# Fused convolution-attention, attention and expert layers: first two weight splits in place, norms and routing later, residual rows and last scatter reordered

## What is computed

```python
# 1: group norm, 1x1 attention over the 1024 points, residual
xn = group_norm(x, 32 groups) * gn_weight + gn_bias
q, k, v = split(qkv_w @ xn + qkv_b)
x = out_w @ (softmax(q.T @ k / 16) @ v.T).T + out_b + xn
# 2: tokens (4, 1024, 256); attention behind residual MLPs
t = tokens(x); n = layernorm(t)
q, k, v = [(n + silu(n @ W1) @ W2) @ aW for each of q, k, v]
t = t + softmax(q @ k.T, over the queries) @ v @ Wout
# 3: mixture of 8 experts, the two likeliest of each token
n = layernorm(t); m = layernorm(n) * ln_g + ln_b
p = softmax(m @ gate_w); c = p where in the top two, else 0
t = t + n + sum_e c[:, e] * (gelu(m @ w1[e] + b1[e]) @ w2[e] + b2[e])
```

## Time and profile before

| what | value |
|---|---|
| median of 3 runs (lowest to highest) | 1194.27 us (1192.0 to 1194.72) |
| profiled execution, its own time | 1192.62 us |
| its span, granted TensorE clock | 1190.9 us, 0.991 |
| PE, DVE, ACT, POOL busy | 95%, 65%, 47%, 21% |
| live expert steps start at, last product ends at | 708.2 us, 1166.2 us |
| HBM traffic over the span | 71 GB/s |

### The profile page before, as it was taken

How to read it: one execution, slowest core, us unless ns; L and a number is a source line. 1 busy time by engine, 2 the same in 40 slices (tenths; PEclk the granted TensorE clock), 3 DMA queues, 4 the chain that set the end, 5 groups by cost and what they waited for, 6 DMA issues and landing times. The chain is left out here.

```text
span 1190.9 us, 24660 instructions
## 1 busy us (share of the span) xinstructions
PE 1137.0 (95%) x8066; PEld 1057.9 (89%) x8067; DVE 777.2 (65%) x1876; ACT 554.1 (47%) x1002; POOL 254.9 (21%) x311
## 2 busy tenths in 40 slices
PE   6999999999999999999999988999899999999995
PEld 5898898888997988998988887998899999999894
DVE  5676376785475676476764679577877667766662
ACT  3533354533343532345433457677666345554442
POOL 3010000100140100231000413236433332323331
PEclk9999999999999999999999999999999999999998
DMA  5001000110010110010000361348675254345338
GB/s 173 1 1 36 1 1 1 37 36 1 15 63 2 36 36 1 33 44 19 18 1 1 108 218 24 58 117 232 198 202 130 48 129 120 61 117 124 56 59 287
DMA packets 70631, 84.65 MB, mean 71 GB/s; under 512 B 11664, under 2 KB 62096, under 8 KB 70544
## 3 DMA queue, kind: packets, MB, share of 16 engines
q1 hardware_dynamic: 57104, 66.22, 17.7%
q0 software_dynamic: 13440, 17.32, 8.1%
HBM read 55.31 MB, written 29.25 MB: 71 GB/s over the span
## 5 line engine op out<-in xcount | busy, mean ns | idle before, releaser
L1719 PE MATMUL ps<-w2s,hs 128*128 128x256 f32 x1728 | 251.1, 280 | 19.2 <-DVE hs L1685 16.2
L1719 PE MATMUL ps<-xt,w1s 128*128 128x256 f32 x1746 | 256.1, 282 | 1.2 <-issue 1.1
L1719 PEld LDWEIGHTS ps<-w2s,hs 128*128 128x128 f32 x1728 | 221.8, 188 | 25.0 <-DVE hs L1685 14.6
L1719 PEld LDWEIGHTS ps<-xt,w1s 128*128 128x128 f32 x1746 | 224.9, 188 | 1.9 <-issue 1.8
L1037 ACT ACTIVATE h<-ps,b1t 128x256 f32<-128x256 f32 x288 | 137.2, 478 | 127.2 <-PE ps L1719 86.2
L771 POOL DMA_INDIRECT acc_rows<-y_w,now_s x72 | 119.0, 1652 | 167.4 <-ACT y_w L1055 112.0
L1683 DVE CAST hs<-h 128x256 fp32r<-128x256 f32 x288 | 87.8, 305 | 95.1 <-ACT h L1037 53.9
L1685 DVE TENSOR_TENSOR hs<-h,hs 128x256 fp32r<-128x256 f32 x288 | 123.6, 429 | 9.9
L1719 PE MATMUL ps<-xs,wh 128*128 128x512 f32 x384 | 121.4, 397 | 1.8 <-issue 1.7
L1719 PEld LDWEIGHTS ps<-vk,pr 128*128 128x128 f32 x768 | 96.2, 190 | 4.7 <-DVE pr L1539 2.5
L1719 PE MATMUL ps<-vk,pr 128*128 128x256 f32 x768 | 97.4, 282 | 1.8 <-DVE pr L1539 1.8
(11 more groups left out here) (248 smaller groups left out, 1725.3 us busy)
## 6 DMA issues: line engine op xcount, KB each, us to landing
w1r<-in_w SPq DMA_DIRECT2D x13, 1024.0 KB
w2r<-in_w SPq DMA_DIRECT2D x13, 1024.0 KB
xg<-sorted_rows SPq DMA_DIRECT2D x38, 272.0 KB
b2t<-in_b SPq DMA_DIRECT2D x37, 128.0 KB
xn<-in_x SPq DMA_DIRECT2D x4, 1024.0 KB, 4.9
acc_rows<-r_out SPq DMA_DIRECT2D x4, 1024.0 KB, 5.1
rows<-acc_rows SPq DMA_DIRECT2D x8, 512.0 KB, 5.6
out_tokens<-cols_out SPq DMA_DIRECT2D x8, 512.0 KB
```

Source lines behind the costliest of these rows:

```text
L1719: ins = t.matmul(out, left[l], right[r], start=first and n == 0, stop=last and n == 2, **more)
```

## The change

1. `w1s`, `w2s` of both sets now lie first in memory; `in_lo` are fp32 names for the places of the four `lo` halves. `whole_weights` loads the weights of steps 0 and 1 straight into them, `in_place` copies `hi` and subtracts in place. `EARLY` splits all 16 pieces in the last image, at chunks 1 to 7; on DVE they stand before `max2(i + 2)` instead of behind it. Step 0 splits nothing (`chunks(i, n, False)`). SP waits for the last scores before it loads into `w1r`, `w2r`, which now lie over `xs`, `qs` and `ks`.
2. `table_a1` and `table_a2` move from chunks 0 and 1 of the last second attention to the projections, between `slots` and `weigh`.
3. The tail's tables in the expert steps move later: statistics from step 0 to 0 and 1, affines from 1 to 1 and 2, the rest by about one step; the sends of sorted rows and six of nine pads too.
4. `stream` of images 0 to 2 moves from before `hi1(0)` and chunk 1 to chunks 1, 2, 5, 6; `tail_stats(b - 1, 1)` from chunk 0 to 1.
5. ACT tests `fresh` in the unrolled steps too.
6. POOL's `scatter(s)` and `note_step(s + 2)` stand at the end of step `s`; before, `scatter(s - 1)` and `note_step(s + 1)` stood there, and the last scatter behind the loop.

```diff
--- before.py
+++ after.py
@@ -246,11 +246,18 @@
-        w1s, w2s = [halves("w1s0", [P, KC, FF])], [halves("w2s0", [P, FC, C])]
+        here = ExitStack()
+        in_lo = []
+        for n in range(4):
+            sb(f"past_hi{n}", [P, KC * FF], F32, here)
+            in_lo.append(sb(f"in_lo{n}", [P, KC * FF], F32, here))
+        here.close()
+        w1s, w2s = [], []
+        for n in range(2):
+            w1s.append(halves(f"w1s{n}", [P, KC, FF]))
+            w2s.append(halves(f"w2s{n}", [P, FC, C]))
         w1r = es("w1r", [P, 2, KC * FF])
         w2r = es("w2r", [P, 2, FC * C])
-        w1s.append(halves("w1s1", [P, KC, FF]))
-        w2s.append(halves("w2s1", [P, FC, C]))
         y_w = es("y_w", [P, 2, SUB, C])
@@ -410,31 +417,33 @@
         CNT = NT * E
-        EARLY = {4: (0, 1), 5: (2, 3), 6: (4, 5), 7: (6, 7)}
+        EARLY = {1: (0, 1), 2: (2, 3), 3: (4, 5, 6), 4: (7, 8), 5: (9, 10), 6: (11, 12, 13), 7: (14, 15)}
...
-        STATS_AT = {(0, 1): 0, (0, 3): 1}
-        NORMAL_AT = {(0, 6): 0, (1, 1): 1}
-        AFFINE_AT = {(1, 1): (0, 0), (1, 2): (0, 1), (1, 5): (1, 0), (1, 6): (1, 1)}
-        TURN_AT = {(1, 5): 0, (2, 0): 1, (2, 3): 2, (2, 6): 3}
-        COLUMNS_AT = {(2, 0): 0, (2, 3): 1, (2, 6): 2, (3, 1): 3}
-        GATE_TILES_AT = {(3, 2): (0, 1), (3, 3): (2, 3), (3, 4): (4, 5), (3, 5): (6, 7)}
-        READ_AT = (3, 7)
-        TOPS_AT = {(4, 0): (0, 1, 2), (4, 1): (3, 4, 5), (4, 2): (6, 7)}
-        CHOOSE_AT = (4, 3)
-        RANKS_AT = (4, 5)
-        EXP_AT = (4, 7)
-        SLOTS_AT = (5, 0)
-        WEIGH_AT = (5, 1)
-        TABLE_AT = {(5, 2): 0, (5, 4): 1, (5, 6): 2, (9, 2): 3}
-        ROWS_AT = {5: (0,), 6: (1, 2, 3), 7: (4, 5), 8: (6, 7)}
+        RESIDUAL_AT = {1: (0, 1), 2: (2, 3), 5: (4, 5), 6: (6, 7)}
+        STATS_AT = {(0, 5): 0, (1, 3): 1}
+        NORMAL_AT = {(1, 2): 0, (1, 7): 1}
+        AFFINE_AT = {(1, 6): (0, 0), (2, 0): (0, 1), (2, 3): (1, 0), (2, 6): (1, 1)}
+        TURN_AT = {(2, 4): 0, (2, 7): 1, (3, 2): 2, (3, 5): 3}
+        COLUMNS_AT = {(2, 7): 0, (3, 2): 1, (3, 5): 2, (4, 0): 3}
+        GATE_TILES_AT = {(4, 1): (0, 1), (4, 2): (2, 3), (4, 3): (4, 5), (4, 4): (6, 7)}
+        READ_AT = (4, 6)
+        TOPS_AT = {(4, 7): (0, 1, 2), (5, 0): (3, 4, 5), (5, 1): (6, 7)}
+        CHOOSE_AT = (5, 2)
+        RANKS_AT = (5, 4)
+        EXP_AT = (5, 6)
+        SLOTS_AT = (5, 7)
+        WEIGH_AT = (6, 0)
+        TABLE_AT = {(6, 1): 0, (6, 3): 1, (6, 5): 2, (9, 2): 3}
+        ROWS_AT = {6: (0,), 7: (1, 2, 3), 8: (4, 5), 9: (6, 7)}
         STREAM_AT = {(4, 0): 0, (4, 2): 1, (5, 1): 2, (5, 5): 3, (6, 1): 4, (6, 5): 5, (7, 1): 6, (7, 5): 7}
-        PADS_AT = {6: (0, 1), 7: (2, 3, 4), 9: (5, 6, 7, 8)}
+        PADS_AT = {7: (0, 1, 2), 8: (3, 4, 5), 9: (6, 7, 8)}
         ROWS_OUT_AT = 8
@@ -518,6 +527,13 @@
+            def whole_weights(n, e):
+                sp.dma_start(in_lo[2 * n][:, :].rearrange("p (k f) -> p k f", k=KC),
+                             w1_d[bass.ds(e, 1)].rearrange("e p k f -> (e p) k f")).then_inc(w1_in[n], 16)
+                sp.dma_start(in_lo[2 * n + 1][:, :].rearrange("p (f c) -> p f c", f=FC),
+                             w2_d[bass.ds(e, 1)].rearrange("e p f c -> (e p) f c")).then_inc(w2_in[n], 16)
@@ -560,13 +576,14 @@
-            weights(0, expert(0))
-            biases(0, expert(0))
+            for n in range(2):
+                whole_weights(n, expert(n))
+            for n in range(2):
+                biases(n, expert(n))
             sp.wait_ge(rows_free, B)
...
             gather(1, 1, True)
-            weights(1, expert(1))
-            biases(1, expert(1))
+            sp.wait_ge(s2_mm, B * NT)
@@ -762,7 +779,7 @@
-            def scatter(s, n, first):
+            def scatter(s, n):
@@ -775,13 +792,11 @@
                     s = i * 2 + n
-                    if not (isinstance(i, int) and s == 0):
-                        scatter(s - 1, 1 - n, isinstance(i, int) and s == 1)
-                    if not (isinstance(i, int) and s == 0):
-                        note_step(s + 1, 1 - n, (i if n == 0 else i + 1))
+                    scatter(s, n)
+                    note_step(s + 2, n, i + 1)
                     if isinstance(i, int):
-                        if s in ROWS_AT:
-                            send_rows(B - 1, ROWS_AT[s])
+                        if s + 1 in ROWS_AT:
+                            send_rows(B - 1, ROWS_AT[s + 1])
@@ -800,7 +815,6 @@
                     steps(i)
-            scatter(final_step(pool), 1, False)
@@ -896,8 +910,6 @@
                 else:
-                    for j in range(4):
-                        stream(b - 1, j)
                     hi1(0)
@@ -906,8 +918,8 @@
                         hi1(i)
-                    if not first and i == 1:
-                        for j in range(4, NT):
+                    if not first:
+                        for j in RESIDUAL_AT.get(i, ()):
                             stream(b - 1, j)
@@ -962,15 +974,21 @@
                         for piece in EARLY.get(i, ()):
-                            w_piece(0, 0, 0, piece)
+                            in_place(piece // 8, piece % 8)
+            def in_place(n, f):
+                if f % 4 == 0:
+                    act.wait_ge((w1_in, w2_in)[f // 4][n], 16)
+                c = slice(f % 4 * 512, (f % 4 + 1) * 512)
+                hi = (w1s, w2s)[f // 4][n][0][:, :, :].rearrange("p a b -> p (a b)")
+                a.copy(hi[:, c], in_lo[2 * n + f // 4][:, c]).then_inc(ws_act, 1)
...
-                first = isinstance(s, int) and s < 2
                 if f % 4 == 0:
                     act.wait_ge((w1_in, w2_in)[f // 4][n], at(u, 16, 16))
-                    if not first:
-                        act.wait_ge((h_mm, y_mm)[f // 4], at(s, FC, -FC))
+                    act.wait_ge((h_mm, y_mm)[f // 4], at(s, FC, -FC))
                 c = slice(f % 4 * 512, (f % 4 + 1) * 512)
@@ -1015,8 +1033,8 @@
                     act.wait_ge(b_in[n], at(i, 32, 32))
-                    if isinstance(i, int):
-                        chunks(i, n, True)
+                    if isinstance(i, int) and s == 0:
+                        chunks(i, n, False)
                     else:
@@ -1056,9 +1074,11 @@
+            act.wait_ge(tab_a, 1)
             for i in range(LOOP_AT):
+                if i == LOOP_AT - 1:
+                    act.wait_ge(tab_b, 1)
                 steps(i)
-            act.wait_ge(tab_b, 1)
             with act.Fori(LOOP_AT, PAIRS) as i:
@@ -1476,7 +1496,7 @@
                         max1(i + 2)
-                    if not first and i == 0:
+                    if not first and i == 1:
                         tail_stats(b - 1, 1)
@@ -1524,6 +1544,9 @@
                             slots(b - 1, RANK_BANK, 0)
+                            if last:
+                                table_a1()
+                                table_a2()
                         if gi == RANK_AT + 2:
@@ -1562,20 +1585,24 @@
                         lo2(i)
+                    if last:
+                        for piece in EARLY.get(i, ()):
+                            in_place(piece // 8, piece % 8)
                     if i + 2 < NT:
                         max2(i + 2)
-                    if last:
-                        if i == 0:
-                            table_a1()
-                        if i == 1:
-                            table_a2()
-                        for piece in EARLY.get(i, ()):
-                            w_piece(0, 0, 0, piece)
                     if not last:
...
+            def in_place(n, f):
+                dve.wait_ge(ws_act, 8 * n + f + 1)
+                c = slice(f % 4 * 512, (f % 4 + 1) * 512)
+                hi, lo = [a[:, :, :].rearrange("p a b -> p (a b)") for a in (w1s, w2s)[f // 4][n]]
+                v.tensor_tensor(lo[:, c], in_lo[2 * n + f // 4][:, c], hi[:, c].bitcast(F32),
+                                ALU.subtract).then_inc(ws_dve, 1)
```

## The result

The changed kernel takes 1195.56 us (median of 19 runs, 1193.21 to 1197.78), the kernel before 1192.00 beside it (19 runs); the measured ratio is 1.0039, interval 1.0029 to 1.0049. (All ratios here are the measured ones with their intervals; the quotient of two medians can differ from them by 0.001, here it is 1.0030.) I had forecast 1187.0 and faster with a chance of 0.83: it is slower than before, and 8.6 us above the forecast. The profiled execution took 1197.78 us, its span 1196.1 against 1190.9 before. It is the slowest of the 19, 2.2 us above the median, so the 5.2 us between the two spans overstate the difference somewhat.

A forecast was written before the change was run, and what follows sets the result against it. PE, busy 95% of the span, was taken as the bound, so only its waits count. The terms summed to -6.2 us, 1192.6 to 1186.4; half a microsecond added gave 1187.0, range 1184.5 to 1191.5 (chance 0.66).

The forecast's parts named there:

- Residual rows: First attention, images 1 to 3: moving the streams removes three PE waits for `lo1`, -2.7 us (0 to -2.7).
- The step table: First scores of the second attention: PE waits +3.0 us for the `u_read` memset, and a lower clock adds +1.6.
- End of the last image: Early splitting of both first weights shortens PE's wait there and keeps the clock up: -2.0 us (+1 to -3.4).
- Steps 0 to 2: First expert steps: less DVE splitting and statistics work cuts PE's loss from 8.7 to about 3, -5.0 us (-2.5 to -7.2).
- Later steps: Routing runs one step later and `table_b` fills step 6, leaving DVE no slack step behind it: +0.5 us (0 to +2).
- sends and pads: Sorted rows and pads move towards step 12, which reads them; the read comes 4.6 us later: +1.0 us (0 to +4).
- rival 3: Step 12's rows a full step late: PE waits 8.0 us and the clock falls, 1195.6 us, slower; chance 0.06.
- The loop: ACT's branch on `fresh` and its dropped copies: both set at 0, bounds -1 and +2.8 us.
- Last scatter: End of kernel: POOL's last scatter issues 0.85 us after the last `y_w` ends, -2.6 us (-2.0 to -2.7).

The follow-up runs named there:

- e4: The kernel before with only POOL's scatter and note moved as in the change; ratio 1.0008 to the kernel before.
- e10: The kernel before with only ACT's branch on `fresh` in unrolled steps 1 to 11; ratio 0.9998 to the kernel before.
- e11: e9 with the nine pads in two groups, five at key 7 and four at key 9; ratio 0.9953 to the kernel before.
- e1: The changed kernel with SP loading step 11's biases ahead of its wait for sorted rows and pads; 0.9994 to the kernel before, 1191.47 us.
- e20: The changed kernel with SP loading biases of step s+1 ahead of rows of step s+2 in every step; ratio 0.9942 to the kernel before.
- e18: e9 with norms, routing, row sends and pads at their old steps, and biases ahead of rows in every step; 0.9903 to the kernel before.
- e15: e9 with biases of step s+1 loaded ahead of rows of step s+2 in every step; ratio 0.9912 to the kernel before.
- e19: e18 with POOL's rotated order of scatter and note; ratio 0.9888 to the kernel before, 1179.89 us.
- e12: e9 with 16 unused register loads on POOL ahead of the loop; ratio 1.0014 to the kernel before.
- e16: e15 with 16 unused register loads on POOL ahead of the loop; ratio 0.9928 to the kernel before.
- e9: The changed kernel with step 11's biases first, the table's first parts behind the memset and POOL's old order; 0.9945 to the kernel before.
- e2: The changed kernel with POOL's sends of sorted rows done by one step earlier; ratio 1.0010 to the kernel before.

## Why the prediction was wrong, by its steps

- **Residual rows, -2.7**: right; alone 3.0 us. The waits for `pr` of the first attention are gone.
- **The step table, +3.0 and +1.6**: right. The rows, as the earlier trace rows, with a window of the products behind the wait:

```profile
651.13 0.06 DVE L1553 MEMSET spare<- 128x1 f32 x1
...
651.35 4.58 PE L1746 MATMUL ps<-qs,ks 128*128 128x512 f32 x12 [2.81 <-DVE spare L1553]
...
652.00:656.00 4.00, 4.00 (x13) 3.13 (x12) 0.03 (x1) 0.00 (x0) 0.00 (x0) 0.57 0.00 0
...
698.36 3.00 PE L1746 MATMUL ps<-vk,pr 128*128 128x256 f32 x24 [0.62 <-DVE pr L1562]
```

PE waits 2.81 (forecast 3.0), and the clock falls to a mean of 0.57 in the window behind: the twelve products take 4.58 us where they took 2.91, 1.7 more (forecast 1.6). Moved behind the memset it gives back 3.6 to 4.3 us of the 4.6 that I had counted.
- **End of the last image, -2.0**: right, rather more. PE's last two waits are 0.62 and 0.49 us where the one of 1.81 stood, and the first group of 24 products behind them took 3.00 us, against 4.60: this is the 2.99 of the full level that I had estimated. The stretch to turn 0 gained 3.7 where -0.1 was forecast; of this up to 2 us is the scatter of the stretch itself: e4 and e10, which change nothing ahead of turn 0, had it at 702.7 and 703.5, before at 704.9.
- **Steps 0 to 2, -5.0 (-2.5 to -7.2)**: -3.6, within the bounds. The early split carries it (2.6), the spreading adds 1.0, less than I gave to the norms. The turns are 10.3, 10.5 and 15.7 us apart, where I had 10.5, 13 and 13: step 1 gives back all, step 2 almost nothing.
- **Later steps, +0.5**: +1.2 up to turn 11. In step 9 it is more (17.4 against 14.5), which I did not work out; e11 points to the full DMA engines. The neighbours give most of it back.
- **The step that failed: sends and pads, +1.0 (0 to +4), with rival 3.** This term looked at the rows alone. I checked when PE turns them, found 3.6 us of slack, and did not follow what else stands behind SP's wait: the biases of step 11, which ACT needs before PE needs the rows. For those there was no slack in the kernel before. Measured against the turns, the read came 6.1 us later than before (I had 4.6). For the rows themselves this costs PE 1.72 us, as e1 shows, near my +1.0; the biases take the rest of the +6.8, and the fall of the clock behind PE's wait 1.9 more in step 12, so that the term measured +8.7. "These sends were never the last to hold anything before" was right of the kernel before, where POOL's note was the last; moved a step later, they were. Rival 3 gives the time almost to a microsecond, 1195.6, but by luck: it has the rows a full step (11.63) late and PE waiting 8.0 for them, while PE waited 6.40, for `hs`, with the rows 6.1 late, and other terms were off as well.
- **The loop, 0**: +4.0, of which 1.9 are step 12, counted above. Most of the rest is at the changes of expert and goes with the order of the loads (e20: 285.2). The row of ACT's waits behind L1025, from which I took 1.5 us for a branch, can hold the wait for the biases too, since this stands in the same queue ahead of the branch: the 9.60 us of step 11 are booked there. The 1.5 itself was no such wait: with the biases first it is 16.8 us over 11 times in e18, 18.1 over 11 in e15 and 9.5 over 7 in e20, 1.4 to 1.6 each. It is idle time of ACT, and taken in more steps it costs the kernel nothing (e10). The Trainium skill (Advanced Engine Details and Errata, Control Flow Timing) gives about 108 ns for a compare-and-branch; the 1.4 to 1.6 us do not agree with it as the price of the whole entry, and no run here takes them apart further.
- **Last scatter, -2.6**: nothing. POOL and ACT at the end of the changed kernel, which answer to the earlier trace rows:

```profile
1165.82 1.66 POOL L788 DMA_INDIRECT acc_rows<-y_w,now_s  x1 [0.30 <-issue]
1174.59 0.19 POOL L778 CAST now_s<-xg 128x2 int32<-128x2 f32 x1 [7.10 <-DMA acc_rows<-y_w,now_s]
1174.71 0.19 POOL L779 COPY now_f<-xg 128x2 f32 x1
1175.65 1.55 POOL L788 DMA_INDIRECT acc_rows<-y_w,now_s  x1 [0.74 <-POOL now_f L779]
...
1171.76 0.91 ACT L1073 ACTIVATE y_w<-y_b,now_f 128x256 f32<-128x256 f32 x2 [5.29 <-DVE y_b L1654]
```

The last `y_w` ends at 1172.67, and the scatter is issued at 1175.65, 0.74 us after the note. The way from the note to the issue is as short as I had estimated. But the note itself waits for the scatter before to land, 7.10 us, and ends 2.2 us after `y_w`. I had taken `y_w` for the last to come, because in the kernel before the note ended at 1167.87, 0.1 us ahead of it; so the note had no slack at all. In the table the end is 3.1 us worse than forecast. In e19 the note is early enough, the scatter goes out at 1155.77, 0.85 us after `y_w` (the estimate exactly), and 1.5 us earlier against the last product than in e18; it then takes 7.02 us to land where e18's takes 6.09, and 0.5 us is left at the end.

## What to carry to other kernels

When work moves later or a stretch before a wait gets shorter, list everything that is queued behind that wait on its engine, with the time at which each is needed; the first to be needed sets the slack, not the one that the wait was written for. A load that depends on nothing late belongs ahead of one that waits for a slow engine, in every step of a loop, not where it showed. A wait that the profile puts down to a sequencer may be the wait that stands ahead of the branch: reorder what it waits for before giving the branch a price.

## What I had not expected of the hardware

- Sixteen register loads on POOL took some 10 us (10.25 us idle ahead of the scatter behind them in e12, 10.31 in e16; without the loads the same scatter went out after 0.81 in e9 and 1.97 in e15), so I estimate about 0.6 us each.
- With all 16 DMA engines busy, PE waited up to 1.1 us at a time with no releaser (steps 9 of e2, e9, e20), and step 9 took 18 to 19 us. In e11, with fewer transfers queued at once in it, it took 13.95. That it is PE's own instructions that come late is only my reading; nothing here shows it.
- PE's idle times of 2.81 and of 6.40 us were both followed by products at the lower level of the clock, for some 3 and 5 us: the granted clock is back at 1.00 in 656 to 658 us and in 875 to 880 us. After 0.62 us of idle time it did not fall (24 products in 3.00 us).
